# A new order of the steps of a slot on all four compute engines, with P times V' directly behind the second pair of V' products

## What is computed

```python
def attn_layer(x, Wqkv, qs, ksc, Wo):
    q, k, v = split(x @ Wqkv)                 # 16 heads of 64
    q, k = l2norm(q) * qs, l2norm(k) * ksc
    q = q * cos * scale + rotate_half(q) * sin * scale
    k = k * cos / scale + rotate_half(k) * sin / scale
    out = local_attention(q, k, v)            # softmax over 2 windows of 32 keys
    return out @ Wo

for i in range(6):
    x = attn_layer(shift_tokens(x), ...) + x
    x = ffn_layer(shift_tokens(x), ...) + x   # layer norm, W1, a * gelu(gate), W2

x = x + 0.5 * ffn_stack(layernorm(x))
x = x + retention(layernorm(x))
x = x + 0.5 * ffn_stack(layernorm(x))
```

## Time and profile before

| | |
|---|---|
| time, median of 3 executions | 3528.91 us (3528.77 to 3534.39) |
| profiled execution, its own time | 3533.1 us |
| its span, first to last instruction | 3531.3 us |
| PE busy | 3402.0 us, 96% |
| DVE busy | 2847.4 us, 81% |
| ACT busy | 2365.6 us, 67% |
| POOL busy | 2333.9 us, 66% |
| mean granted TensorE clock | 0.984 of 2.4 GHz |

### The profile page before, as it was taken

The page is one execution under the profiler, slowest core; times in us unless marked ns, Lnnn a source line. Parts: engine busy times, 40 slices in busy tenths (PEclk is TensorE's granted clock), DMA queues, the critical chain, the costliest instruction groups (busy, mean ns, idle before and its releaser), DMA issues.

```text
span 3531.3 us, 123143 instructions
## 1 busy us (share of the span) xinstructions
PE 3402.0 (96%) x51660; PEld 1851.7 (52%) x51660; DVE 2847.4 (81%) x6052; ACT 2365.6 (67%) x4133; POOL 2333.9 (66%) x2187
## 2 busy tenths in 40 slices
PE   6999999999999999999788999999999999999996
PEld 3555555555555555555354555555555555555553
DVE  6888888888888888886468888888888888888883
ACT  3676677667677667767424777677767767767764
POOL 5766667676677677775137777677677677667761
PEclk8999999999999999999998999999999999999998
DMA  2001001001001001000100000000000000000000
GB/s 83 11 14 47 12 14 47 13 15 47 12 14 47 13 14 35 9 12 20 38 2 23 14 23 22 17 23 22 12 29 22 12 27 23 12 27 10 12 5 13
DMA packets 49223, 76.64 MB, mean 22 GB/s; under 512 B 7072, under 2 KB 37024, under 8 KB 47136
## 3 DMA queue, kind: packets, MB, share of 16 engines
q1 hardware_dynamic: 48672, 68.76, 6.1%
HBM read 61.39 MB, written 7.34 MB: 19 GB/s over the span
## 4 chain that ended last, share of the span: by engine, by line
PE 93%; DVE 3%; issue 2%; POOL 1%; ACT 1%; DMA 0%; SPq 0%; DVEq 0%; POOLq 0%; ACTq 0%
PE VS L902 20%; PE QA L838 19%; PE TB L857 10%; PE TB L926 9%; PE VS L952 8%; PE TB L881 6%; PE FB L980 4%; PE FB L989 4%; PE FB L981 4%; PE VS L936 2%; PE TB L865 1%; PE FB L965 1%; PE FB L970 1%; DVE T L608 1%; POOL QN L343 0%
## 5 line engine op out<-in xcount | busy, mean ns | idle before, releaser
L343 POOL TENSOR_TENSOR QN<-T 128x512 f32<-128x512 f32 x768 | 979.9, 1276 | 578.6 <-DVE T L608 578.6
L350 POOL TENSOR_TENSOR QN<-QN,RR 128x512 f32<-128x512 f32 x768 | 800.7, 1043 | 296.9 <-DVE RR L629 296.9
L838 PE MATMUL QA<-WQ,Y 128*128 128x512 f32 x1536 | 797.8, 618 | 20.2 <-DVE T L608 12.1
L902 PE MATMUL VS<-MW,Y 128*32 128x512 f32 x6144 | 741.8, 600 | 5.0 <-DVE Z L691 5.0
L451 ACT ACTIVATE SQ<-QA 128x512 f32<-128x512 f32 x768 | 458.8, 597 | 294.0 <-PE QA L838 268.7
L608 DVE TENSOR_TENSOR T<-QA,TAB 128x256 f32<-128x256 f32 x1536 | 570.7, 412 | 0.0
L603 DVE TENSOR_TENSOR T<-QA,TAB 128x512 f32<-128x512 f32 x768 | 513.6, 669 | 38.1 <-ACT SQ L451 23.2
L471 ACT ACTIVATE V<-VS 128x512 f32<-128x512 f32 x768 | 461.0, 600 | 95.1 <-PE VS L902 94.5
L926 PEld LDWEIGHTS TB<-CST,QN 128*128 128x128 f32 x3072 | 374.2, 142 | 256.8 <-issue 191.6
L359 POOL TENSOR_TENSOR Z<-Z,RC 128x512 f32<-128x512 f32 x384 | 394.5, 1048 | 142.8 <-DVE RC L671 142.8
L616 DVE TENSOR_REDUCE SSQ<-SQ 128x8 f32<-128x512 f32 x768 | 487.2, 676 | 0.0
(11 more groups left out here) (166 smaller groups left out, 4206.0 us busy)
## 6 DMA issues: line engine op xcount, KB each, us to landing
TAB<-in_tables SPq DMA_DIRECT2D x192, 128.0 KB, 2.1
WQ<-in_w_qk SPq DMA_DIRECT2D x48, 256.0 KB, 2.9
m_dram<-MW SPq DMA_DIRECT2D x6, 1024.0 KB, 5.4
MW<-m_dram SPq DMA_DIRECT2D x6, 1024.0 KB, 5.2
W1R<-in_w SPq DMA_DIRECT2D x12, 341.0 KB, 3.0
WS<-in_w_vt SPq DMA_DIRECT2D x6, 512.0 KB, 5.9
WS<-in_w_out SPq DMA_DIRECT2D x6, 512.0 KB, 7.8
W<-in_w SPq DMA_DIRECT2D x12, 192.0 KB, 2.4
```

Of the source, the lines that this page charges most:

```text
L343: po.tensor_tensor(QN[:, n % 2, k, :], T1[:, k, :], T2[:, k, :], ALU.add).then_inc(s_add, 1)
L350: po.tensor_tensor(heads(QN[:, m % 2, k, :]), heads(QN[:, m % 2, k, :]), RR[:, m % 2, 8 * k:8 * k + 8].unsqueeze(2).to_broadcast([P, 8, DH ...
L838: mm(QA[:, k % 2, :], Y[:, j * P:(j + 1) * P], WQ[:, k, :], start=True, stop=True).then_inc(s_qk, 1)
L902: last = mm(VS[32 * q:32 * q + 32, w % 2, :], Y[:, a:a + WIN], MW[:, l % 2, q, :], start=True, stop=True, tile_position=(0, 32 * q), skip_ ...
```

## The change

The steps are the same, their order in a slot is another on all four engines, and one DVE instruction has another form.

- PE: `project_qk(1)` comes directly behind `project_qk(0)`; `attend` moves from ahead of the transposes of P to behind V2 and V3; `out_transpose` to between k2 and k3; the weight fold (first stack only) behind the transposes of q and k.
- ACT: both squares come first, then the copy of P, the softmax Exp, and only then V0 and V1; the copy of O moves behind V3; the Ln and Exp of the norms move ahead of the copy of P at the slot's end.
- DVE: `inverse_norm` moves ahead of row maxima and subtraction; the residual moves from the slot's end into its middle, and now serves tile c-5 instead of c-4 (the same product, since before it waited for PE's next slot).
- POOL: the scaling of parts 2 and 3 of tile c-1 is done earlier.
- DVE's lower bound of the norms, `tensor_scalar_max(NRM, SSQ, 1e-24)`, becomes a `tensor_tensor` maximum with a constant tile TINY of 128x32, filled once.

The diff's core:

```diff
@@ scalar @@
-                if live(c, 5, it):
-                    m = n - 5
-                    ac.wait_ge(s_o, by_tile(1, m, it, 1))
-                    nc.scalar.activation(ON[:, m % 2, :], TB[:, 1, 0:P], ACT.Copy).then_inc(s_oe, 1)
+                if live(c, 0, it):
+                    square(0)
+                    square(1)
                 if live(c, 4, it):
                     p_out(4, 1)
-                    v_out(0)
...
+                if live(c, 4, it):
+                    v_out(0)
+                    v_out(1)
                 if live(c, 1, it):
                     qk_out(1, 0)
                     qk_out(1, 1)
                 if live(c, 4, it):
                     v_out(2)
+                    v_out(3)
+                if live(c, 5, it):
+                    m = n - 5
+                    ac.wait_ge(s_o, by_tile(1, m, it, 1))
+                    nc.scalar.activation(ON[:, m % 2, :], TB[:, 1, 0:P], ACT.Copy).then_inc(s_oe, 1)
                 if live(c, 0, it):
                     square(2)
...
                     qk_out(1, 2)
-                if live(c, 3, it):
-                    p_out(3, 0)
                 if live(c, 0, it):
                     ac.wait_ge(s_rm, by_tile(1, n, it, 1))
...
+                if live(c, 3, it):
+                    p_out(3, 0)
@@ vector @@
+                if live(c, 5, it):
+                    ve.wait_ge(s_ot, by_tile(1, n - 5, it, 1))
+                    attn_residual(*HALVES[0])
+                    attn_residual(*HALVES[1]).then_inc(s_res, 1)
                 if live(c, 0, it):
                     rotate(2)
                     square_sum(2)
                     square_sum(3)
                     ve.wait_ge(s_red, by_tile(4, n, it, 4))
-                    nc.vector.tensor_scalar_max(NRM[:, n % 2, :], SSQ[:, n % 2, :], 1e-24).then_inc(s_rm, 1)
+                    nc.vector.tensor_tensor(NRM[:, n % 2, :], SSQ[:, n % 2, :], TINY[:, :], ALU.max).then_inc(s_rm, 1)
                 if up1_g is not None:
                     hidden(up1_g, 1)
                 if live(c, 0, it):
                     rotate(3)
+                    inverse_norm()
                 if live(c, 2, it):
...
-                if live(c, 0, it):
-                    inverse_norm()
...
-                if live(c, 4, it):
-                    ve.wait_ge(s_ot, by_tile(1, n - 4, it, 1))
-                    attn_residual(*HALVES[0])
-                    attn_residual(*HALVES[1]).then_inc(s_res, 1)
@@ tensor @@
                     project_qk(0)
                 if up2_g is not None:
                     ffn_up(up2_g, 2)
-                if live(c, 5, it):
-                    attend()
+                if live(c, 0, it):
+                    project_qk(1)
                 if live(c, 4, it):
                     p_transpose(4, 1)
                     project_v(0)
                     project_v(1)
-                if live(c, 5, it):
-                    out_transpose()
-                if fold_piece(c, s):
-                    fold_weights(*fold_piece(c, s))
-                if live(c, 0, it):
-                    project_qk(1)
                 if live(c, 1, it):
                     qk_transpose(1, 0)
                     qk_transpose(1, 1)
+                if fold_piece(c, s):
+                    fold_weights(*fold_piece(c, s))
                 if live(c, 4, it):
                     project_v(2)
                     project_v(3)
+                if live(c, 5, it):
+                    attend()
                 if live(c, 0, it):
                     project_qk(2)
                 if up2_g is not None:
                     ffn_down(0)
+                if live(c, 5, it):
+                    out_transpose()
```

More of the change, by code:

```diff
@@ L114, in build_macaron @@
         LNB = sb("LNB", [P, 1])
+        TINY = sb("TINY", [P, 32])
         RST = sb("RST", [P, 24])
@@ L326, in _ @@
             po.memset(LNB[:, :], 8.0 * 0.6931471805599453).then_inc(s_cst, 1)
+            po.memset(TINY[:, :], 1e-24).then_inc(s_cst, 1)
             def slot(c, it, s):
@@ L374, in slot @@
                     norm_mult(1, 1)
+                    norm_mult(1, 2)
                 if live(c, 0, it):
@@ L377, in slot @@
                 if live(c, 1, it):
-                    norm_mult(1, 2)
+                    norm_mult(1, 3)
                 if live(c, 0, it):
@@ L382, in slot @@
                     softmax_mult()
+                if live(c, 0, it):
+                    rot_add(2)
                 if live(c, 2, it) and (c - 2) % 4 == 3:
                     last_keys()
-                if live(c, 0, it):
-                    rot_add(2)
-                if live(c, 1, it):
-                    norm_mult(1, 3)
                 if live(c, 0, it):
@@ L554, in stack @@
                 all_slots(ac, slot, s)
-            ac.wait_ge(s_cst, 5)
+            ac.wait_ge(s_cst, 6)
             ac.preload_act_table_set("natural_log_exp_and_others")
@@ L632, in attn_residual @@
                 def attn_residual(rows, one):
-                    m = n - 4
+                    m = n - 5
                     a = (m % TPL) * P + one
@@ L671, in slot @@
                     nc.vector.reciprocal(RC[:, m % 2, :, :], SM[:, m % 2, :, :]).then_inc(s_rc, 1)
+                if fold_piece(c, s):
+                    l, p = fold_piece(c, s)
+                    ve.wait_ge(s_mp, 4 * (l - 1) + p + 1)
+                    if l >= 2:
+                        ve.wait_ge(s_ms[l % 2], 16 * (l // 2))
+                        ve.wait_ge(s_vp, 4 * TPL * (l - 1))
+                    nc.vector.tensor_copy(
+                        MW[:, l % 2, 2 * (p % 2):2 * (p % 2) + 2, :].rearrange("p q (e c n) -> p e c q n", e=2, c=2)
+                        [:, :, p // 2, :, :], FB[:, :, 0:2 * P].rearrange("p e (q n) -> p e q n", q=2)).then_inc(s_mo, 1)
+                if live(c, 5, it):
+                    ve.wait_ge(s_ot, by_tile(1, n - 5, it, 1))
+                    attn_residual(*HALVES[0])
+                    attn_residual(*HALVES[1]).then_inc(s_res, 1)
                 if live(c, 0, it):
@@ L739, in pads @@
                 nc.vector.memset(Y2[64:128, 0:1], 0.0)
-            ve.wait_ge(s_cst, 5)
+            ve.wait_ge(s_cst, 6)
             pads()
@@ L845, in attend @@
                         after(pe, s_res, 1, n - 6, 0, it, s)
-                    after(pe, s_te, 3, n - 2, 2, it, s)
+                        after(pe, s_te, 3, n - 2, 2, it, s)
+                    after(pe, s_te, 3, n - 1, 1, it, s)
                     for b in range(CH):
@@ L915, in qk_transpose @@
                         if edge:
-                            after(pe, s_te, 3, n - 2, 2, it, s)
+                            after(pe, s_res, 1, n - 6, 0, it, s)
+                        after(pe, s_te, 3, n - 2, 2, it, s)
+                    elif k == 2:
+                        if edge:
+                            pe.wait_ge(s_te, by_tile(3, m, it, 2))
                         after(pe, s_res, 1, n - 5, 0, it, s)
-                    elif k == 2:
-                        pe.wait_ge(s_te, by_tile(3, m, it, 2))
                     else:
```

20 lines of the change are left out of this document (removed).

## The result

The changed kernel takes 3723.83 us (median, 3718.80 to 3725.52); the kernel before, on the same chip, 3529.88 us. The ratio is 1.0545, with a 95% interval of 1.0526 to 1.0563. The forecast had the direction, and by most of its steps the mechanism; it said +125 us, and it was +194. The measured time lies outside the range.

What follows compares the result with a forecast made beforehand. PE, busy 96% of the span, was taken to set the time. Per round of A to D, 3.65 us of stalls less 1.04 won, 2.6 net, made +125 us in 48 rounds: 3655 us, range 3587 to 3712.

Steps and rivals of the forecast that it cites:

- The stall of V0, with ACT's RN as its cause: PE in slot C: V0 waits for DVE's subtraction, itself late for ACT's RN behind the gelu; 2.24 us a slot C.
- What PE saves: PE, each slot: `attend` behind V2/V3 drops one change of column form; 0.26 us a slot, 50 us in all.
- the rival of 3705: PE: the passage from V' to `attend` costs a full change of form, so the saving is lost; 3705 us, 13 in 100.
- `inverse_norm` 0.63: DVE, ahead of row maxima and subtraction in its new place: `inverse_norm` takes 0.63 us.
- "0.2" in A: Slot A: DVE's chain and V0 come out on a par, ACT's RN may add a little; 0.2 us of stall.
- in B nothing: Slot B: no stall of V0, since slot A's tail has a 0.86 us variance product behind the scores and no gelu.
- The bound of the norms: DVE's lower bound of the norms as `tensor_tensor`: 0.2 us, taken from LA's 0.18, saving some 0.8 us into DVE's idle time.
- The clock: Rival: gaps of 2.2 us each round bring PE to the lower clock, 120 us over 48 rounds; near 3775 us, 3 in 100.
- one of the prediction's own signs of being wrong: Changed profile: wrong if LA never waits, V' to `attend` takes 1.85 or more, or the clock is below 1.00 mid-stack.
- The rival of the table drain: Rival: each ACT table switch drains, RN 1.38 us later, stalls of C and D 1.4 larger each; 3790 us, 1 in 100.
- The other side: Rival: the wait for RN is hidden, V0 is never late and PE keeps its 50 us; 3479 us, 7 in 100.
- D's 1.2 us: PE in slot D: 0.5 us stall of V0, plus 0.25 and 0.45 behind ACT's copies; together 1.2 us.

Runs made afterwards that it cites:

- the kernel with POOL's wait: The changed kernel with POOL's add of the halves of the fourth rotation waiting until DVE has written RR: 3645.81 us, ratio 1.0318.
- the filler: The changed kernel with two spare matmuls of 384 columns on PE ahead of V0 in most slots C, product never read: 3698.36 us, ratio 1.0469.
- all the edits above together: The changed kernel with POOL's wait, norms ahead of gelu, ACT's copies first, fewer or later table loads, and C's `hidden` behind `inverse_norm`: 3481.67 us, ratio 0.9870.
- the copies alone: The changed kernel, ACT's copies of V0, V1, first two transposes ahead of softmax Exp, in D P's copy ahead of squares: 3718.62 us, ratio 1.0530.

## Why the prediction came out as it did

Mean slot lengths over both stacks, after less before: A +0.35, B +0.31, C +2.24, D +0.94 us a round, 3.83 in all; the forecast was 2.6, as A -0.06, B -0.26, C +1.98, D +0.94. The difference of 1.23 makes 59 us in 48 rounds, of the 69 by which the forecast missed. The other 10 lie outside the whole slots, at the stacks' ends, and were not followed. The 1.23 is itself a balance: waiting beside POOL adds 1.33 in A and B, the falls of the clock 0.55 in C, and the forecast's other terms, held against the kernel with POOL's wait, were some 0.65 too high (0.26 in A, 0.10 in B, 0.30 in C).

**The stall of V0, with ACT's RN as its cause: right.** Gelu, table load, QT, Ln, Exp, LA, maxima, subtraction, V0 follow one another as listed. PE idles 1.86 us in a C at full clock, and the slot, at 17.83 (forecast 18.0), is 2.14 longer than a B without stalls (forecast 2.24). The experiment in which POOL's add waits shows this part clean.

**What PE saves: right, and a little more.** 0.26 us a slot was forecast; B without stalls is 15.69, 0.34 under before. The passage from V' to `attend` costs all but nothing, 1.75 us for the pair where 1.72 stood for free and 1.85 for a change of form, so the rival of 3705 falls.

**The step that failed: "`inverse_norm` 0.63", and with it "0.2" in A and "in B nothing".** That term, from the earlier trace rows, was mis-sized for its new place: 0.63 us where 1.5 to 1.7 was measured. In the kernel before, `inverse_norm` came behind maxima and subtraction, when POOL had nothing running but in 4 of 192 cases, and only in those 4 did an LA take over 194 ns. Behind `rotate(3)` it stands where POOL begins the add for the part that `rotate(3)` has just delivered. There 138 of 384 LA instructions take 1.02 to 1.27 us, and so `inverse_norm` with one of them takes 1.5 to 1.7 us. The prediction went through who is queued behind it, but not through who runs beside it. At the median it puts 0.87 us into A (16.80 against 15.93) and 0.70 into B (16.38 against 15.68); over all slots of both stacks the mean is 0.67 in each. V0 of C isn't touched, since RN comes later there than the add. The 44 long ones at the start of D do delay V0 there, but without them PE waits nearly as long for ACT's copies, so D keeps its length (19.54 with them, 19.53 without). The added wait on POOL gives back 78 us.

The mechanism, as far as runs show it: the held instructions are those with two inputs in SBUF (LA, both forms; NRM with TINY), and NRM's `tensor_scalar` in the kernel before; their ends follow POOL's add by 0.04 to 0.05 us; ordering that add behind LA leaves no long LA. No semaphore of POOL stands ahead of these instructions. DVE instructions with an input in PSUM and the reductions with one input show nothing like it: in the changed kernel the sum of squares (L614) takes 0.67 to 0.68 us in all 576 cases in which it starts beside a running POOL instruction. The Trainium skill, "SBUF — State Buffer", section "Who interferes with whom", states it: a DVE instruction with two SBUF inputs contends with a GpSimd instruction that reads SBUF, and the one that starts second is blocked until the first has ended. By that rule the trace agrees, 1.26 us beside an add of 1.27. Weighed against the change's new neighbours, it would have foretold the stall.

**The bound of the norms: right value, wrong reason.** 0.2 us was forecast from LA by the form, and 0.19 measured; but with the form alone it is 986 ns, so that it came out is luck. The earlier trace rows held the clue to the failed step: a least of 181 and a median of 979 ns for the same instruction is not a price; the 979 hold a wait.

**The clock: a rival at 3 in 100 that came in part.** It was priced for all rounds (3775) and dismissed by a stretch with 2 of 5 us idle at full clock. It came in 14 of the 42 slots C, at 1.64 us each (2.5 in the rival), some 25 us by the filler. One stretch that kept its clock was weak evidence against a gap repeated 48 times. With POOL's wait it came in 19. A clock below 1.00 in the middle of a stack was one of the prediction's own signs of being wrong.

**The rival of the table drain: fell.** QT starts 0.01 us behind the table load, as before.

**The other side:** "PE keeps its 50 us, 3479" is not what the change does, but what it needs for it is now shown: with all the edits above together it takes 3481.67. That it is so near 3479 is chance, for it is not 0.26 us in each slot: B and C are 0.34 shorter than before, A 0.05, and D 0.08 longer.

**D's 1.2 us: right in total, by luck in the changed kernel.** The forecast's net of 0.94 is what was measured (0.94 on the mean, 0.99 at the median), but there it is all but wholly V0's wait, 1.20 us in the slot shown. The forecast's parts (0.5 for V0, 0.25 and 0.45 behind ACT's copies) are seen with POOL's wait only: 0.35, 0.46 and 0.27, 1.08 together.

What stays open: what the kernel with `inverse_norm` behind again waits for beyond POOL's QN; what happens at the stacks' ends; and in the fastest kernel, the table loads against `hidden`'s place.

## What to carry to other kernels

When an instruction is moved, ask what runs beside it in its new place on the other engines, not only what queues behind it; here a short DVE instruction with two SBUF inputs that started beside POOL's add cost the rest of that add. A row whose least and median lie five times apart, as 181 and 979 ns do, may hold a wait inside the instruction's duration, and its cause should be found before its median or its least is used in a sum. A total that fits proves little: here D's length and the bound of the norms came out right for reasons the forecast did not have. A stall is rarely removed at one place: of the edits in the fastest kernel, the norms ahead of the gelu alone only moved the stall to the next slot and the copies alone gave nothing, but with POOL's wait in place they, the fewer table loads and the later `hidden` took the ratio from 1.0318 to 0.9870.
